# Splitting the shared-expert additions between GpSimd and VectorE differently at the end of an expert kernel: four tiles kept instead of two

## The reference, cut to what matters

```python
x = x + ga * attention(h, w_qkv, w_out)
h = layernorm(x) * (1 + cb) + sb
w, idx = top-4 of 16 per token                    # the router
y = sum over the 4 experts of  c * ((silu(h @ Wg.T) * (h @ Wu.T)) @ Wd.T)
z = (silu(h @ Sg.T) * (h @ Su.T)) @ Sd.T          # the shared expert
return x + gb * (y + z)
```

## Time and profile before

| | us |
|---|---|
| median of 3 runs | 631.28 |
| lowest and highest | 627.23 and 631.92 |
| span of the profiled execution, first to last instruction and transfer | 630.8 |
| TensorE busy in it | 520.9 (83%) |
| shared stage: from its first matmul to the end | 561.7 to 630.8 |

### The profile page before, as it was taken

The page is one execution under the profiler, slowest core; times in us unless marked ns, Lnnn a source line. Parts: engine busy times, 40 slices in busy tenths (PEclk is TensorE's granted clock), DMA queues, the critical chain, the costliest instruction groups (busy, mean ns, idle before and its releaser), DMA issues. The chain is left out here.

```text
span 630.8 us, 13294 instructions
## 1 busy us (share of the span) xinstructions
PE 520.9 (83%) x3587; PEld 490.1 (78%) x3588; DVE 402.5 (64%) x1154; ACT 279.1 (44%) x740; POOL 298.4 (47%) x337
## 2 busy tenths in 40 slices
PE   1597991899999999999853068799999999999897
PEld 0287891799998898898842057699998999998896
DVE  3697731323568768769777199677776777774543
ACT  1252542223644544635325274355554555553232
POOL 5644520200104446445566499634443444447893
PEclk9798996557999999999955559799999999999899
DMA  7135688427776458462275653244443444446931
GB/s 221 47 110 171 209 211 244 130 70 177 193 173 182 143 143 215 129 168 75 94 234 197 234 181 94 69 125 127 125 125 110 128 134 127 124 143 249 415 146 51
DMA packets 63668, 98.41 MB, mean 156 GB/s; under 512 B 10084, under 2 KB 48867, under 8 KB 62263
## 3 DMA queue, kind: packets, MB, share of 16 engines
q1 hardware_dynamic: 50504, 58.37, 34.3%
q0 software_dynamic: 9184, 32.66, 13.8%
q10 hardware_dynamic: 3918, 6.67, 3.3%
HBM read 60.84 MB, written 40.17 MB: 160 GB/s over the span
## 5 line engine op out<-in xcount | busy, mean ns | idle before, releaser
L1572 POOL DMA_INDIRECT ys_scr<-h,ids_st x60 | 61.6, 1027 | 73.5 <-DVE h L1626 71.2
L109 PE MATMUL GU<-gu_hi,xT 128*128 x320 | 86.9, 354 | 5.2 <-DVE lo L1655 3.1
L144 POOL DMA_INDIRECT xs_scr<-h,slot_u x64 | 62.4, 975 | 55.7 <-PE TB L1194 26.7
L109 PE MATMUL YP<-dn_hi,aT 88*128 x320 | 69.1, 308 | 4.9 <-DVE aT L1611 4.8
L1618 DVE TENSOR_TENSOR h_act<-GU,g_act 128x176 f32<-128x176 f32 (+1 forms) x96 | 35.5, 370 | 57.2 <-ACT g_act L1490 56.2
L1204 PE MATMUL O<-raw,prob 128*128 128x99 f32 x512 | 71.2, 289 | 0.0
L823 ACT ACTIVATE prob<-TB 128x512 f32<-128x512 f32 x64 | 38.2, 597 | 71.5 <-PE TB L1194 70.7
L1497 ACT ACTIVATE aT<-HT 88x256 fp32r<-88x256 f32 (+1 forms) x96 | 38.1, 398 | 69.5 <-PE HT L1728 69.4
L1204 PEld LDWEIGHTS O<-raw,prob 128*128 128x128 f32 x512 | 66.7, 205 | 0.0
L109 PEld LDWEIGHTS GU<-gu_hi,xT 128*128 128x128 f32 x320 | 54.3, 198 | 6.3 <-issue 6.3
L109 PEld LDWEIGHTS YP<-dn_hi,aT 88*128 88x128 f32 x320 | 49.1, 191 | 11.2 <-issue 7.2
(11 more groups left out here) (226 smaller groups left out, 1291.2 us busy)
## 6 DMA issues: line engine op xcount, KB each, us to landing
x_st<-xs_scr SPq DMA_DIRECT2D x80, 144.0 KB
dn_hi<-k_scr SPq DMA_DIRECT2D x48, 192.0 KB, 3.8
planes<-ys_scr POOLq DMA_DIRECT2D x8, 1024.0 KB, 17.4
k_scr<-k_ev SPq DMA_DIRECT2D x8, 768.0 KB, 4.8
dn_hi<-q_scr SPq DMA_DIRECT2D x24, 256.0 KB, 4.4
q_scr<-q_ev SPq DMA_DIRECT2D x8, 512.0 KB, 3.0
raw<-in_egu SPq DMA_DIRECT2D x8, 352.0 KB
raw<-in_x SPq DMA_DIRECT2D x36, 64.0 KB, 2.7
```

The lines of the kernel that those rows point to most:

```text
L109: mm = eng.matmul(out, a, b, start=(i + j == 0), stop=(i == len(pairs) - 1 and j == 2))
L144: eng.indirect_dma_start(T["xs_scr"], bass.IndirectOffsetOnAxis(ap=T["slot_u"][:, par, t % 2, k:k + 1], axis=0), T["h2"][:, row, :], None) ...
L1572: eng.indirect_dma_start(ys, bass.IndirectOffsetOnAxis(ap=ids_st[:, r:r + 1].bitcast(U32), axis=0), results(r % 8), None).then_inc(sent[q] ...
```

## The change

Four tiles (two pairs, g = 0 and 1) are kept instead of two. GpSimd folds 12 tiles instead of 14. The planes of the kept pairs are loaded last instead of first; x of tiles 4 to 7 is loaded second, behind one load of planes, instead of third. VectorE's additions of the kept pairs are spread out: one instruction a round at the round's end, for pair 0 in rounds 10, 11 and 12, for pair 1 in rounds 13, 14 and 15. The stores go in the new order in which the pairs are finished.

```diff
-    KEPT = 2
-    LOADED = (1, 0, 2, 3, 4, 5, 6, 7)
+    KEPT = 4
+    LOADED = (2, 3, 4, 5, 6, 7, 0, 1)
+    STORED = (2, 3, 4, 0, 5, 6, 1, 7)
+    ADDS = (10, 13)
...
-        for k, g in enumerate(LOADED):
+        for k, g in enumerate(STORED):
             eng.wait_ge(final, k + 1)
             store_out(g)
...
         for n, g in enumerate(LOADED):
             load_planes(eng, g)
-            if 1 <= n <= 3:
-                load_add(eng, n)
+            if n % 2 == 0 and n < 6:
+                load_add(eng, n // 2 + 1)
...
-        def add_kept(k, g):
+        def add_kept(g, part):
             at = slice(2 * g, 2 * g + 2)
-            eng.wait_ge(four_ld[g], 16)
-            eng.tensor_tensor(planes[:, at, 0:2, :], planes[:, at, 0:2, :], planes[:, at, 2:4, :], ALU.add).then_inc(z_fold, 1)
-            eng.wait_ge(z_fold, 2 * k + 1)
-            eng.tensor_tensor(planes[:, at, 0, :], planes[:, at, 0, :], planes[:, at, 1, :], ALU.add).then_inc(z_fold, 1)
-            eng.wait_ge(z_fold, 2 * k + 2)
-            eng.wait_ge(z_late, KEPT)
-            eng.tensor_tensor(to_add[:, at, :], to_add[:, at, :], planes[:, at, 0, :], ALU.add).then_inc(final, 1)
+            if part == 0:
+                eng.wait_ge(four_ld[g], 16)
+                eng.tensor_tensor(planes[:, at, 0:2, :], planes[:, at, 0:2, :], planes[:, at, 2:4, :], ALU.add).then_inc(z_fold, 1)
+            elif part == 1:
+                eng.wait_ge(z_fold, 2 * g + 1)
+                eng.tensor_tensor(planes[:, at, 0, :], planes[:, at, 0, :], planes[:, at, 1, :], ALU.add).then_inc(z_fold, 1)
+            else:
+                eng.wait_ge(z_fold, 2 * g + 2)
+                eng.wait_ge(z_late, KEPT)
+                eng.tensor_tensor(to_add[:, at, :], to_add[:, at, :], planes[:, at, 0, :], ALU.add).then_inc(final, 1)
...
-            if n == KEPT + 3:
-                add_kept(0, 0)
+            for g in range(KEPT // 2):
+                if ADDS[g] <= n < ADDS[g] + 3:
+                    add_kept(g, n - ADDS[g])
```

## The result

The changed kernel takes 624.78 us (median of 20 runs, 617.20 to 627.43), the kernel before 629.19 us (median of 20 runs, 620.83 to 631.92, the three of the prediction among them). The ratio is 0.9935, with a 95% interval of 0.9908 to 0.9961: faster by 0.65%, that is 4.1 us (2.5 to 5.8), and within the 1% that was called no clear change. Ratios and their intervals leave out the slow runs of each kernel, those more than 1.5% above its fastest. The runs of one kernel spread by 10 to 11 us, more than the whole effect; so what follows measures the shared stage inside the traces, where the same round repeats to a hundredth of a microsecond.

A forecast was written before the change was run, and what follows sets the result against it. TensorE, the busiest engine, was taken to lose 5.33 us in rounds 4 to 9. Span 630.8 - 5.33 + 0.9 (late planes) + 0.3 (other parts) = 626.7; median 0.5 above, 627.2 us; range 623.2 to 630.4.

The forecast's parts named there:

- the three losses: TensorE in rounds 4 to 9: 1.39 us late first fold, 2.39 wide additions before `gating`, 1.55 low clock; all go.
- GpSimd's first fold: Tile 4's fold, done at 582.4 or 585.7 at the latest, wanted by VectorE in round 6 at 586.05; costs nothing.
- The planes of pair 0: Round 10: loaded late and delayed 1.6 us by stores, they land at 602.3 (600.7 to 603.4); TensorE loses 0.9 us.
- the row of h2: Profile row: one 128 KB h2 load on SyncE's queue served within five microseconds while planes were queued; taken to support stores overtaking.
- The sign named for it: In the timeline after, `gating` of round 11 is about 1 us late, with a wait for the planes' transfer before it.
- What a part costs: VectorE's additions in rounds 10 to 15: free up to 1.67 us, lengthened by waits for GpSimd's instruction; five parts cost 0.3 us.
- The tail: Round 15 and after: VectorE has 1.4 us for part 2, and the last store still sets the kernel's end.
- The sum: Whole kernel: 630.8 - 5.33 + 0.9 + 0.3 = 626.7 us span; median 0.5 above, 627.2.
- the forecast's own range: Whole kernel's time in the forecast case: 625.8 to 629.0 us, chance 0.50.
- a lower level of the runs: Whole kernel: runs after lie at the lower of the levels seen in three runs, giving 623.1 us; chance 0.12.
- Everything is hidden: Rounds 10 to 15: stores do not delay pair 0 and parts meet GpSimd at good moments; 626.0 us, chance 0.20.
- the slow rival: Round 10: pair 0 lands at 606, TensorE pauses 4.6 us, low clock adds 1.55; 632.4 us, chance 0.04.

The follow-up runs named there:

- Experiment 3: Changed kernel with the parts one round earlier: round 4's gate-up to end 54.56 us, against 50.2; two rounds earlier 57.7 and 57.9, timed ratio to kernel before 1.0153.
- experiment 2: Changed kernel with each pair's three additions in one round (12 and 15): round 4's gate-up to end 55.3 us, repetition 53.9, against 50.2; repetition's timed ratio 1.0045.
- experiment 4: Changed kernel with SyncE's first store held until pair 1's planes landed: round 4's gate-up to end 51.1 us; pair 0 landed 24.0 after issue instead of 23.7.
- Experiment 7: Changed kernel with GpSimd leaving out the folds of tiles 10 to 15: round 4's gate-up to last addition 47.15 us, against 47.34.
- experiment 1: Kernel before with only pair 0's additions spread over rounds 10 to 12, two tiles kept, old loads: round 4's gate-up to end 54.8 us, against 55.3.
- experiment 5: Changed kernel with the kept pairs' planes loaded first: 629.51 us, ratio to kernel before 1.0038; round 4's gate-up to end 56.45 us.
- experiment 6: Changed kernel with two more GpSimd additions behind its last fold, awaited by nobody: to last addition 47.35 us, span end 3.3 us later than without.

## Why the prediction was right

- **What bounds, and what goes: right.** All 5.33 us of the three losses went, round by round. Experiment 3 shows that pauses of TensorE are followed by the low clock at 1.4 us a time, as in round 7 before; but it is no fixed rule of the pause, since 2.67 us in the repetition of experiment 2 were not, and in experiment 4 the clock fell behind 0.98 us.
- **GpSimd's first fold: right.** x landed at 571.0 + 6.8 = 577.8, on the clock of before 580.1 against the estimated 579.5. VectorE wanted the fold 2.9 us after it was done.
- **The planes of pair 0: the term that was mis-sized.** The step "that is 0.13 + 0.26 + 0.26 = 0.65 MB more before the planes are in" gave a landing at 602.3 and a loss of 0.9. It landed at 601.15 on that clock, within the bounds, and the loss was 0. The stores do get turns, as the Trainium skill says (DMA: Bandwidth & Descriptors, "Queues, rings and completion order"): 90 packets beside 93 in 594 to 596. But I had taken a turn for a share of the bytes; the row of h2 on which I leaned has 130 packets for 0.12 MB, so it already showed turns of 1 KB. Experiment 4 shows no effect of the stores. The sign named for it, `gating` of round 11 late by 1 us with a wait for the planes before it, did not come; the others did (rounds of 3.54, no low clock, no wait of `to_add` for GpSimd).
- **What a part costs: right in mechanism, high in its mean.** The six parts took 5.95 together, 0.8 over their bare lengths, where I expected 0.5 for each of four. Part 0 of round 13 begins at 609.87 and ends 1.09 behind 610.48, the end of GpSimd's second instruction. That fits the exclusive lock of which the Trainium skill speaks (SBUF — State Buffer, "SBUF: two separate sides"), held for a whole instruction. Experiment 7 takes the waits away. The cost was 0.2 against 0.3, from the one part that was expected to exceed 1.67. That the parts lengthen GpSimd's folds as well, by 2.9 us in all, was no term of the prediction: it had the folding end near 614, and it ended at 617.6 on that clock, still running beside part 1 of round 14.
- **The tail: right by luck.** GpSimd's drain was no part of the working. Before the change it ended 1.3 us ahead of SyncE's wait for the last store. Now the two ends fall together within 0.1 us, so the trace does not tell whether "the last store still sets the end"; had GpSimd ended later by more than that, the end would have moved with it, as in experiments 1, 5 and 6.
- **The sum.** Predicted 4.1 us of gain; the stage shows 5.15. The 1.0 between them is the planes' 0.9 that did not come and 0.1 on the parts. The timed ratio gives 4.1 (2.5 to 5.8) and can't tell the two apart. The predicted 627.2 stood on a median of three runs, 631.28, which with twenty is 629.19; that is 2.1 of the 2.4 us between 627.2 and 624.78. So 624.78 lies below the forecast's own range of 625.8 to 629.0, and it is within the whole range because that was opened downward for a lower level of the runs. That part of the hit is luck. The 0.5 us by which the median was said to lie above the span compared different executions: where both are on record, a run's time is 1.9 above its own span.
- **The rivals.** "Everything is hidden" is nearest to the traces (5.15 of 5.33), and was given 0.20. Experiment 3 made the slow rival's mechanism happen near the price named for it: 1.4 us for the clock, where 1.55 was named.

## What to carry to other kernels

A stall taken out of a pipelined stage is worth what the next latest partner leaves of it: experiments 1 and 5 lost half of the gain to waits and lengths that the old stall had covered, and the rest or nearly so to GpSimd's later end. An engine that is off the critical path can still set the end of the kernel. Work for an idle gap of an engine should be cut to the gap (here 1.33 us of idle time and 0.3 around it), counting a wait for the partner's running instruction, rather than be put into the round with the most room. When two queues share full transfer engines, count packets, not only bytes, and look at how long the small transfers of the other queue take.

## What the runs showed of the hardware that was not expected

- GpSimd's drain at the end of the last block: 8.61 to 8.63 us in eight of the fourteen traces, 8.9 to 9.6 in five where its last instruction was itself lengthened by VectorE. In all these it ends 7.8 to 7.9 us behind that instruction. The traces that ended with it ended 8.0 to 8.1 us behind GpSimd's last instruction, and the wait is credited to TensorE's queue. Only in experiment 7, with no instruction running when it began, was it 9.5 with no such cause; why is open.
- The clock behind a pause of TensorE: 2.15, 2.52, 2.88, 6.11 and 6.25 us of pause were followed by a round of 4.9 to 5.1 us at a mean granted clock of 0.65 to 0.69. Pauses of 1.14 (before, experiment 1), 1.75 (experiment 5) and 2.67 us (experiment 2, repeated) were not. In experiment 4 the clock was 0.50 behind the 0.98 us that nearly every tail has, and it cost 1.0 us. So the same kernel can have this cost or not, and the length of the pause alone does not say which.
- With the transfer engines full, a 256 KB store of SyncE's queue took 7.3 to 8.0 us to land, and 2.0 us once the loads were in.
